# Early-fusion transformer stages on one core: fourteen images per loop turn in place of two

## What is computed

```python
h = _L0_tok_ref(x, curve, proj_w, proj_b)                       # 256 tokens of each image
h = jnp.concatenate([h, _L0_txt_ref(x_txt, mask, ...)], axis=1) # and 128 of text
h = h + _L0_attn_ref(_layernorm(h), Wq, Wkv, ...)    # 12 heads, rotary
h = h + _L0_ffn_ref(_layernorm(h), router_w, ...)    # 5 experts, all computed, two weighted
h = h + _L1_attn_ref(_layernorm(h), qA, qB, kA, ...) # 6 heads, causal, low rank
h = h + _L1_ffn_ref(_layernorm(h), Wg, W1, W2)       # 8 experts, top 2, with a capacity
```

## Time and profile before

| | |
|---|---|
| runs of the kernel before | 4902.61, 4910.84, 4916.66 us; median 4910.84 |
| the profiled execution | 4902.13 us, of which the span of instructions is 4900.3 us |
| busy share of the span | PE 92%, PEld 72%, DVE 59%, ACT 48%, POOL 37% |
| filling bodies | 42 to 375 us |
| loop of 14 turns, 2 images each | 375 to 3629 us, 232.5 us a turn |
| draining bodies | 3629 to 3910 us |
| expert part | 3910 to 4900 us |

### The profile page before, as it was taken

One profiled execution on the slowest core, in us unless ns is written; L12 is line 12 of the kernel. 1 busy time (PEld: TensorE's weight loads), 2 busy tenths in 40 slices (PEclk: granted clock), 3 DMA queues, 4 the chain that ended last, 5 costly groups with the idle time before them and its releaser, 6 DMA issues. The chain is left out here.

```text
span 4900.3 us, 81562 instructions
## 1 busy us (share of the span) xinstructions
PE 4511.4 (92%) x28994; PEld 3522.1 (72%) x28994; DVE 2879.5 (59%) x8068; ACT 2340.5 (48%) x4826; POOL 1836.1 (37%) x1975
## 2 busy tenths in 40 slices
PE   3799999999999999999999999899999599999998
PEld 1566666767666666666666666676766499999998
DVE  4466666666666756566666666666665344444443
ACT  1354554555555555555545455455555233333333
POOL 2123233333232323232233323233321166666666
PEclk7699999999999999999999999999999799999999
DMA  8600000000000000000000000000000111222210
GB/s 145 100 8 13 10 10 10 10 10 10 10 12 10 10 10 10 10 12 10 10 10 15 10 10 10 10 10 10 10 10 9 34 40 38 55 64 55 64 42 14
DMA packets 128566, 116.55 MB, mean 24 GB/s; under 512 B 31311, under 2 KB 119910, under 8 KB 128166
## 3 DMA queue, kind: packets, MB, share of 16 engines
q1 hardware_dynamic: 92774, 74.16, 6.9%
q0 software_dynamic: 35392, 36.93, 2.8%
HBM read 70.73 MB, written 76.16 MB: 30 GB/s over the span
## 5 line engine op out<-in xcount | busy, mean ns | idle before, releaser
L725 ACT ACTIVATE probs<-bank_a 128x384 f32<-128x384 f32 (+2 forms) x1728 | 691.4, 452 | 756.3 <-PE bank_a L823 485.6
L1071 DVE TENSOR_REDUCE neg_max<-bank_v 128x1 f32<-128x352 f32 (+3 forms) x1728 | 777.9, 492 | 224.1 <-PE bank_v L796 146.2
L597 POOL TENSOR_TENSOR rstd<-ve,pow_half 128x3 f32<-128x3 f32 x128 | 111.2, 868 | 1466.9 <-DVE ve L1010 1466.6
L796 PE MATMUL bank_v<-heads_t 49*128 49x352 f32 (+4 forms) x1728 | 403.5, 404 | 65.5 <-DVE neg_max L1071 54.0
L1560 DVE TENSOR_TENSOR e_hid<-e_bank_v,gated 128x384 f32<-128x384 f32 x320 | 178.6, 558 | 481.5 <-PE e_bank_v L1438 481.5
L842 PE MATMUL bank_o<-probs,v 128*32 128x384 f32 (+3 forms) x3456 | 450.4, 491 | 2.5 <-ACT probs L725 0.2
L819 PE MATMUL bank_a<-heads_t 49*128 49x384 f32 (+3 forms) x1728 | 404.2, 397 | 34.2 <-ACT probs L725 32.5
L796 PEld LDWEIGHTS bank_v<-heads_t 49*128 49x128 f32 (+1 forms) x1728 | 210.5, 191 | 278.6 <-DVE neg_max L1071 112.0
L642 POOL DMA_INDIRECT xs_dram<-xn_z,slot_i x192 | 187.2, 975 | 559.6 <-DVE slot_i L1143 510.9
L950 PE MATMUL bank_a<-ffn_x,w_ffn 128*128 128x384 f32 x1600 | 374.3, 366 | 0.0
L950 PE MATMUL bank_v<-ffn_x,w_ffn 128*128 128x384 f32 x1600 | 352.1, 351 | 4.9 <-DVE hid L1216 4.9
(11 more groups left out here) (237 smaller groups left out, 9380.9 us busy)
## 6 DMA issues: line engine op xcount, KB each, us to landing
xs_dram<-zeros SPq DMA_DIRECT2D x30, 780.0 KB, 19.4
rows<-xs_dram SPq DMA_DIRECT2D x240, 97.5 KB
out_tokens<-h_z SPq DMA_DIRECT2D x32, 288.0 KB, 2.3
raw<-in_w SPq DMA_DIRECT2D x8, 512.0 KB, 4.0
raw<-in_w SPq DMA_DIRECT2D x16, 256.0 KB, 5.2
sofar<-out_tokens,token POOLq DMA_INDIRECT x240, 2.2
out_tokens<-res,token POOLq DMA_INDIRECT x240
xs_dram<-xn_z,slot_i POOLq DMA_INDIRECT x192
```

Of the source, the lines that this page charges most:

```text
L725: act.activation(probs[:, n % NPROBS, i, lo:T], empty("score", k, g, kt, i)[:, lo:T], ACT.Exp, scale=DHS[k] ** -0.5).then_inc(a_free, 1)
L796: mm = pe.matmul(bank[:, 0:keys], heads_t[k][r:r + rows, b, tile[t]], heads_t[k][r:r + rows, 6 + b, 0:keys], start=True, stop=(k == 0))
L1071: dve.tensor_reduce(neg_max[k][g % 2][:, t, at:at + 1], bank[:, 0:keys], AX.X, ALU.max, negate=True).then_inc(v_free, 1)
```

## The change

```diff
@@ schedule
-    order = [(s, next(todo[s])) for s in (ORDER_OF_ONE if len(active) == 1 else ORDER)]
+    order = [(s, next(todo[s])) for s in ORDER * (len(active) // 2) + ORDER_OF_ONE * (len(active) % 2)]
@@ body
+            def first_z(r):
+                return isinstance(image_z, int) and image_z + r == 0
+
@@ body, gpsimd, "stats"
-                            if k == 3 and had("z", r):
+                            if k == 3 and not first_z(r):
                                 pool.wait_ge(scattered, (image_z + r) * (16 * 2 * NT))
@@ body, gpsimd, after the units
-                    if nth["z"][-1]:
-                        last = max(r for r, on in enumerate(active) if "z" in on)
-                        pool.wait_ge(scattered, (image_z + last + 1) * (16 * 2 * NT))
+                    if not isinstance(image_z, int) or image_z + len(active) < B:
+                        return
+                    pool.wait_ge(scattered, B * (16 * 2 * NT))
@@ the calls
-        body(["w", "wx"], 0, None, range(n_zero // 2))
-        body(["wxy", "wxyz"], 2, -1, range(n_zero // 2, n_zero))
-        with nc.Fori(0, (B - 4) // 2) as trip:
-            body(["wxyz", "wxyz"], trip * 2 + 4, trip * 2 + 1)
-        body(["xyz", "yz"], None, B - 3)
-        body(["z"], None, B - 1)
+        body(["w", "wx", "wxy", "wxyz"], 0, -3, range(n_zero))
+        with nc.Fori(0, (B - 4) // 14) as trip:
+            body(["wxyz"] * 14, trip * 14 + 4, trip * 14 + 1)
+        body(["xyz", "yz", "z"], None, B - 3)
```

## The result

The changed kernel takes 4872.7 us (median, 4870.5 to 4876.9) where the kernel before takes 4910.1 us beside it: ratio 0.9931, interval 0.9912 to 0.9949. It is faster, by 37 us; I had predicted 82 us and a range that ended at 4850. Two later sets of runs with both kernels gave 0.9939 (0.9924 to 0.9953) and 0.9937 (0.9921 to 0.9952).

A forecast was written before the change was run, and what follows sets the result against it. PE bounds the kernel, busy 4511 of 4900.3 us. Gains of 72.4 + 1.3 + 1.9 + 6 = 81.6 us off the median of 4910.8 give 4829 us; range 4807 to 4850, with the forecast itself between 4815 and 4850 at 0.80.

The forecast's parts named there:

- The seam's idle time: At twelve joined loop returns PE would idle 1.86 us instead of 7.89, gaining 6.03 us each, 72.4 us.
- The clock term: Behind joined seams, one microsecond of low clock would fall on idle time: 0.5 us each, 6 us; ends -11 and +26.
- Rival 1: Clock stays up at the joined seams, giving 26 us instead of 6: 4809 us, chance 0.09.
- The kept seams: Fill to loop, between the two turns, loop to drain, end of token part: four of eighteen stay, entered without change.
- The last draining seam: Between the `yz` and `z` steps, PE could start at 3828.75 instead of 3830.64: 1.9 us gained.
- The first filling seam: In the fill, a barrier without branch back; PE could start at 148.96 instead of 150.21: 1.3 us gained.
- the moved wait: POOL's wait for landed rows, moved from the body's end to `stats` of the next step, never has to wait: 0 us.
- the zeros: SP's thirty writes of zeros become one series in the fill: 0 us, with 6 us as a bound.
- Rival 3: The long straight body starves PE of instructions, so the change is slower, up to 5655 us; chance 0.03.
- Rival 4: The change doesn't do what it says; held excluded at the seams by program order, no chance of its own.
- Rival 2: Smaller gain of 59 us, 4852 us: low clock lasts longer at joined seams, one fetch exposed in the fill; chance 0.07.

The follow-up runs named there:

- set 3: Kernel before and changed kernel, each with matmuls that nobody reads at four places of an image: 4944.0 us (0.9976) and 4879.5 us (0.9839).
- filled_seam: Changed kernel with five matmuls that nobody reads in PE's pause at each joined seam: ratio 0.9888 to the kernel before.
- Set 4: Runs side by side: kernel before 4906.8 us, changed kernel 4876.2, changed kernel with a POOL drain in each image 4857.1; also the fastest version, 4792.9.
- z_apart: Changed kernel with the last image's z step as a body of its own again: ratio 0.9877 to the kernel before.
- sets 2: Both kernels unedited again, ratios 0.9997 and 0.9939, beside changed kernels with matmuls that nobody reads: 45 in the last pause 0.9930, everything combined 0.9799.
- set 1: First follow-up runs: changed kernel with a POOL drain in every image, 0.9865; also in one body, 0.9849; that drain in the kernel before, 0.9966.

## Why the prediction was wrong

**The seam's idle time** (12 x 6.03 us) was right at the seam: 7.6 to 8.3 us, 7.89 on average, became 1.88. Between the stores that enclose the twelve joined seams (2 to 14 and 16 to 28) the first two traces have 2790.5 and 2742.8 us, 47.7 us less. PE's idle time there fell from 170.7 to 103.9 us, 5.6 a seam and not 6.03: the 5.6 us of the 72.4 that are missing are idle time elsewhere in the pairs, for a cause that is not shown. In set 3 a seam gave 6.1 us in the step shown and 6.9 to 7.7 on average.

**The clock term** had the wrong sign. I took 0.5 us a seam on top of 6.03; measured, a seam gave 4.0 (4.2 over three traces of each kernel). Of the 31 us that are missing at the seams, 19 are PE's own busy time, which rose from 2619.9 to 2638.9 us for the same work, 6 are the gain that I had entered, and the rest is the idle time above. The step that failed is the sentence that one microsecond of the low level falls on idle time. It looked at the 8 us from PE's return and not at the 8 us ahead of it. These two stretches of the kernel before:

```profile
1064.00:1072.00 8.00, 0.54 (x5) 0.30 (x3) 2.23 (x9) 0.68 (x1) 0.00 (x0) 0.63 0.01 3
2426.80:2658.90 232.10, 218.18 (x1434) 158.04 (x1432) 150.37 (x455) 123.39 (x252) 73.26 (x82) 0.94 0.04 11
```

In the first, the seam, the clock is 0.63: 8 x 0.37 x 2 = 5.9 us of the low level in which PE worked for 0.54 us. They cost next to nothing. The second is a pair of images; the same in the changed kernel:

```profile
2404.80:2633.30 228.50, 219.85 (x1434) 159.07 (x1432) 150.44 (x455) 123.38 (x252) 73.27 (x82) 0.94 0.04 11
...
601.00:605.00 4.00, 3.37 (x16) 3.26 (x17) 1.63 (x5) 0.97 (x2) 0.00 (x0) 0.57 0.00 0
```

The mean clock is the same 0.94, with 27 us low in either pair, but the cheap ones are gone: idle time fell by (232.1 - 218.2) - (228.5 - 219.85) = 5.3 us and busy time rose by 1.7 us. Over the twelve seams, each low stretch held against PE's matmuls: 69 us of low clock lay on PE's idle time before and 16 after, and 273 us lay on its work before and 312 after. Those 39 us more, at the 0.5 us each that the prediction read, are the 19 us. A low stretch still stands at the joined seam (0.57 over 601 to 605), and in the changed kernel another one has come up some 67 us after every second store; why it comes up there is not shown. I had this as the lower end of the term, but as a loss of 0.9 us a seam, and only for the stretch at the seam itself. The Trainium skill (TensorE: Matmul & The Clock Gate, "Why this matters for your kernels") asks that longer pauses of PE than this one be avoided, or the low clock comes back. As a rule that nothing shorter goes with it, it doesn't fit this trace: each joined seam has a low stretch of 3.4 us beside a pause of 1.88 us. Whether that pause brings it on is not shown, since with the pause filled (filled_seam) six of the twelve seams lost the low stretch and six kept it. Rival 1 is out.

**The kept seams** were entered at nothing ("stay, four of eighteen"). Their drains cost 7.85 us more at the return and at the exit, 0.3 us more at the end of the fill, and the last one 1.0 us more, since it now has the scatters of three images behind it. Set 4 measures the whole of it as 19.1 us less when POOL drains in each image. The step that failed here is a term entered at nothing: the barrier's cost was treated as fixed per seam, while its drain depends on what POOL had issued since the last one, 9.20 us after 112 indirect DMAs. The drains of before add up to 21.7 us (18 of them) and those after to 21.1 us (4). The term of 1.35 us per seam inside the 6.03 was only postponed. It could have been read: in the trace of before the drain takes 374 ns at the first seam, 854 at the second and 1352 at the loop's.

**The last draining seam** (1.9 us gained) was wrong by 9 us: PE's pause did shorten, from 11.59 to 9.7 us, but the low clock behind it lasted 61 us in place of 41. By z_apart and the other traces it goes with this seam. Why the low clock then lasts longer is not settled; that spread work shortens it is shown in one trace.

**The first filling seam, the moved wait, the zeros:** 0.8 us in the fill for 1.3, and no new wait of POOL or DVE before L600 or L1170; right.

**Rival 3** (starved of instructions) is refuted twice: in the token part PE waits for "issue" once for 15.5 us, at the return, and otherwise 0.7 us at most in the changed kernel, and 1.3 us at most in a body of 35 steps without a loop. Rival 4 is out. Rival 2, 4852 us, came nearest and had the clock's direction right, but the result lies beyond it, and of a fetch exposed in the fill no sign is there.

The account: 81.6 predicted, less 31 (the joined seams), 17 to 19 (drains) and 9 (last step), leaves 23 to 25 us; the first two traces differ by 25.3 us, the pairs of traces of sets 2 and 4 by 36 and 41 us, the medians by 30 to 37 us. That spread is left. It goes with the low clock: up to the last store the first and the third trace of before have 594 and 620 us of it, and the third is 12.7 us longer.

## What to carry to other kernels

A barrier is not a fixed price: before merging loop turns, look at what each engine has outstanding when it reaches it, and drain early, under idle time, what would otherwise be drained on the path. When idle time is taken from an engine whose clock is throttled, see first how much of the low clock lies on the idle time itself; here most of that part turned into slow work, and the mean clock of the whole didn't show it. Work that nobody reads, put into pauses, together with one body and the last step apart, was worth 64 us on top of the inner drains, more than the change itself; in the kernel before, where the seams stayed, the same matmuls gave only 14 us.

## What was new of the hardware

- POOL's drain took 374 ns after 4 indirect DMAs since the last drain, 527 after 6, 1196 after 14, 1352 after 16, 2663 after 32 and 9202 after 112: (9202 - 1352) / 96 = 82 ns each and some 40 ns. A drain in the middle of an image took 0.97 us with no DMA behind it and 1.60 with 8: the same 0.08 us each, and some 0.9 us more that this line doesn't give.
- PE's taken branch cost 3.3 to 4.0 us whatever the body's length (3375 ns at a body of fourteen images, 3592 median at two).
- In a step with one stream alone PE ran for 61 us at the low clock with 70.8 us of its 90.5 busy; filling the pause ahead of it changed nothing, and with 36 matmuls spread over it 55 us of low clock became 31, one trace each.
- The ratio of one edited kernel differed between sets by 0.003 (inner drain: 0.9865 in set 1 and 0.9895 in set 4), so ratios of different sets are not to be compared closer than that.
- A low stretch that lies on PE's idle time costs next to nothing: at the seam of the kernel before, 5.9 us of low clock held 0.54 us of PE's work.
